# A two-layer graph network in one kernel: the transposes of the next tile behind a third of the present tile's products

## What is computed

```python
h = relu(layernorm(x))
x = x + gat(relu(gat(h, W1, ...)), W2, ...)     # graph attention, softmax over incoming edges
h = relu(layernorm(x))
x = x + gcn(relu(gcn(h, V1, ...)), V2, ...)     # graph convolution, normalized by degree
```

## Time and profile before

| what | value |
|---|---|
| median of 3 runs | 2283.92 us (2281.28 to 2285.07) |
| profiled execution: its time | 2278.45 us |
| profiled execution: its span | 2276.7 us |
| mean granted TensorE clock | 0.992 of full speed |
| TensorE (PE) busy | 2212.1 us, 97% |
| weight loads (PEld) busy | 1428.2 us, 63% |
| DVE busy | 1520.7 us, 67% |
| ACT busy | 935.1 us, 41% |
| POOL busy | 904.6 us, 40% |

### The profile page before, as it was taken

One profiled execution on the slowest core, in us unless ns is written; L12 is line 12 of the kernel. 1 busy time (PEld: TensorE's weight loads), 2 busy tenths in 40 slices (PEclk: granted clock), 3 DMA queues, 4 the chain that ended last, 5 costly groups with the idle time before them and its releaser, 6 DMA issues.

```text
span 2276.7 us, 36746 instructions
## 1 busy us (share of the span) xinstructions
PE 2212.1 (97%) x13888; PEld 1428.2 (63%) x13888; DVE 1520.7 (67%) x3352; ACT 935.1 (41%) x1291; POOL 904.6 (40%) x1071
## 2 busy tenths in 40 slices
PE   6999999999999999999999999999999999999997
PEld 3666666666666666666666666666665666666664
DVE  6888885444577776334589999766555657885564
ACT  3333433333455445433454444433333333333442
POOL 2332325754233331134455454444334423344562
PEclk8999999999999999999999999999999999999999
DMA  4433334565455554343565566676766657775562
GB/s 141 154 118 106 111 112 113 113 127 202 160 195 190 186 188 167 124 167 119 192 209 184 195 207 207 200 250 241 244 241 205 222 185 237 247 252 178 181 208 82
DMA packets 125668, 407.32 MB, mean 179 GB/s; under 512 B 21993, under 2 KB 22151, under 8 KB 125364
## 3 DMA queue, kind: packets, MB, share of 16 engines
q1 hardware_dynamic: 85124, 232.38, 30.5%
q0 software_dynamic: 40368, 172.60, 24.4%
HBM read 232.32 MB, written 179.87 MB: 181 GB/s over the span
## 4 chain that ended last, share of the span: by engine, by line
PE 80%; DVE 8%; POOL 4%; issue 4%; DMA 2%; ACT 2%; SPq 0%; POOLq 0%; ACTq 0%; DVEq 0%
PE ps_h L893 67%; PE ps_z L876 8%; DMA edge_mem<-rows,pos_dst 2%; PE ps_e L960 1%; PE ps_e L961 1%; DVE z_lo L1106 1%; DVE bn L1054 1%; POOL out L604 1%; DVE edge_mem L1136 1%; DVE res L1125 1%; ACT row_out L782 1%; POOL edge_mem L599 1%; DVE res L1115 1%; POOL rstd L613 1%; PE ps_e L968 0%
## 5 line engine op out<-in xcount | busy, mean ns | idle before, releaser
L893 PE MATMUL ps_h<-w_hi,z_hi 128*128 128x384 f16 x3792 | 928.4, 327 | 0.4 <-DVE w_lo L1045 0.4
L893 PE MATMUL ps_h<-w_lo,z_hi 128*128 128x384 f16 x3792 | 928.2, 327 | 0.0
L893 PE MATMUL ps_h<-w_hi,z_lo 128*128 128x384 f16 x3792 | 927.9, 326 | 0.0
L1106 DVE TENSOR_TENSOR z_lo<-ps_z,z_hi 128x768 f16<-128x768 f32 x316 | 301.7, 955 | 484.5 <-ACT z_hi L787 483.8
L893 PEld LDWEIGHTS ps_h<-w_lo,z_hi 128*128 128x128 f16 x3792 | 371.5, 98 | 246.4 <-issue 1.9
L893 PEld LDWEIGHTS ps_h<-w_hi,z_lo 128*128 128x128 f16 x3792 | 371.5, 98 | 246.0 <-issue 1.4
L893 PEld LDWEIGHTS ps_h<-w_hi,z_hi 128*128 128x128 f16 x3792 | 371.3, 98 | 223.6 <-issue 19.9
L782 ACT ACTIVATE row_out<-ps_h,grow 128x768 f32<-128x768 f32 x237 | 212.9, 898 | 637.7 <-PE ps_h L893 628.1
L876 PE MATMUL ps_z<-ident,z 128*128 128x128 f32 x1896 | 261.0, 274 | 24.8 <-ACT z L795 23.6
L611 POOL TENSOR_SCALAR veps<-mv 128x1 f32<-128x1 f32 x158 | 87.5, 554 | 457.2 <-DVE mv L1057 441.9
L787 ACT ACTIVATE z_hi<-ps_z 128x768 f16<-128x768 f32 x316 | 253.8, 803 | 15.4 <-PE ps_z L876 15.4
(11 more groups left out here) (213 smaller groups left out, 2131.1 us busy)
## 6 DMA issues: line engine op xcount, KB each, us to landing
rows<-row_out SPq DMA_DIRECT2D x199, 384.0 KB, 3.9
row_in<-in_x SPq DMA_DIRECT2D x78, 384.0 KB, 3.6
rows<-e_out SPq DMA_DIRECT2D x60, 384.0 KB, 4.5
row_in<-rows SPq DMA_DIRECT2D x40, 384.0 KB, 4.3
x_rows<-pre SPq DMA_DIRECT2D x40, 384.0 KB, 3.2
res<-x_rows SPq DMA_DIRECT2D x40, 384.0 KB, 4.1
pure_rows<-row_out SPq DMA_DIRECT2D x39, 384.0 KB, 3.5
row_in<-pure_rows SPq DMA_DIRECT2D x39, 384.0 KB, 4.6
```

What stands on the lines that cost most here:

```text
L893: last = nc.tensor.matmul(ps_h[s][:, a, 0:HALF], zp[s][:, c, :], wp[:, c, a * HALF:(a + 1) * HALF], start=(c == 0 and zp is z_hi and wp is ...
L1106: V.tensor_tensor(pair3(z_lo[t.slot]), psum_pair(ps_z), pair3(z_hi[t.slot]), ALU.subtract).then_inc(z_lo_ready, 1)
```

## The change

In `window(w)` of TensorE the call of `turn` for tile w+1 is taken from the front of the window and put into `side_step(0)`, which runs after chunk 1, so behind 12 of the 36 product matmuls of tile w. It stands ahead of all else that `side_step(0)` does. Only where a window has no product (w = -1) it stays in front. Nothing else is edited; ACT, DVE, POOL and SP have the same instructions in the same order.

```diff
             def window(w):
-                if t := tile(w, 1):
-                    turn(t)
                 gat = gat_of(w)
+                after = tile(w, 1)
+                if after and not tile(w, 0):
+                    turn(after)
 
                 def side_step(k):
+                    if after and k == 0:
+                        turn(after)
                     if ORDER <= w < ORDER + ET and k == 1:
                         mask_rows(w - ORDER)
```

## The result

| | before | after |
|---|---|---|
| median | 2284.49 us (4 runs, 2281.28 to 2285.3) | 2354.72 us (4 runs, 2353.89 to 2356.54) |
| ratio | | 1.031, 95% interval 1.029 to 1.033 |
| profiled execution: its time | 2278.45 us | 2354.51 us |
| profiled execution: its span | 2276.7 us | 2352.8 us |
| mean granted clock | 0.992 | 0.991 |

The changed kernel is 3.1% slower: 70 us by the medians, 76.1 by the spans of the two profiled executions. The work is the same; what came is nearly all waiting. Lines of the edited file from 931 on stand three higher than before (L948 is L951, L960 is L963, L968 is L971, L1106 is L1109).

The account below looks back on a forecast made before the run. TensorE, busy 97% of the span, was taken as the bound, so only waits could change. Stage terms summed to +70.5 us on the profiled 2278.45, giving 2349; the median stands 5.5 higher, so 2354, range 2325 to 2382.

Parts of the forecast that it names:

- Rank ring: Rank window pairs: 3.64 us to `z_lo`, 9.77 of DVE, 1.11 to products: 14.52 against 13.64; stage sum +17.8 us.
- The wait in window 28: Special rank pair: the 3.40 us wait for `z` becomes 1.7 without loss of clock; -3.6 us.
- Masks: 20 windows: the mask matmul's input follows `z_lo`, ready at 5.13 us, due at 4.56; wait 0.57 each, +11.4 us.
- First attention layer: 20 pairs, window B: slack before the matmul needing the weights falls from 2.1 to 0.6 us; cost 0 if that holds.
- Second attention layer: 20 pairs where DVE is full: cycle 15.93 us against 14.63 in nine pairs, others differ; +21 us, bounds +12 and +25.
- the recurrence: Second attention layer: DVE's cycle from window A's late `z_lo` to the next window, carried pair by pair; gives 22 us.
- Last edges: 20 windows, the first needing no copy: 19 waits of 0.67 us less some 1 us absorbed; +12 us.
- Plain edges: 20 windows: `carry` copies behind `z_hi` on ACT cost 0.7 us each, partly absorbed by old gather waits; +5.9, at most +14.
- Start: The second tile's transposes, which filled a wait for the first weights, now stand among the products; +0.9 us.
- The two other waits for `z`: Waits for `z` outside the other stages, 3.7 us: due 1.95 later, they fall by 0.9 and 1.95; -2.9 us.
- the weighing in the prediction: Skill's rule on short idles swinging TensorE's clock, set against waits of 1.23 and 1.65 us without half clock: trace disagrees.
- the rival of the falling clock: TensorE's clock falls in half of about 100 new waits, 2.7 us each: +135 more, 2490 us; chance 0.05.

Follow-up runs that it names:

- the second trace of the kernel before: The kernel before, unchanged, profiled once more at the end of the experiments; that execution took 2282.23 us.
- At two thirds: The changed kernel with the transposes behind 24 products, at `side_step(1)`, instead of 12; one execution of 2782.41 us.
- the dots-first kernel: The changed kernel with the first two dot products ahead of `low_parts` on DVE in window A of the second attention layer; span 2335.8 us.
- the carry-first kernel: The changed kernel with ACT's `carry` (plain edges) and `last_carry` ahead of `upper_parts`; span 2329.5 us.
- all reorderings: The changed kernel with `mask_diag`, statistics and two dot products ahead of `low_parts`, carries ahead of `upper_parts`, window 0's transposes in front; 2280.25 us, ratio 0.9986.
- Behind a sixth: Transposes behind 6 products in all windows but window 0, with the four queue reorderings, against the kernel before; 2281.61 us, ratio 0.9993.

## Why the prediction was right, point by point

**The sum.** +70.5 predicted on the profiled execution, +76.1 in the profiled execution after, +70 by the medians; 2354 us against 2354.72. That the last two agree to 1 us is luck: by the profiles I was 5.6 us short, and the two profiled executions stand at different distances from their medians (6.0 under, 0.2 under). Against the second trace of the kernel before the shift is 72.3.

**Rank ring: right.** 9.77 us of DVE and 3.64 us of lateness gave 14.52 a pair, measured 14.41. Statistics ahead of `low_parts` opened the ring. The wait in window 28 was worked out as 1.7 us, measured 1.55, without loss of clock, as forecast. Where the rows would show it I had partly wrong: L893 waits for `z_lo` 8 times and not 20, most of the pair's wait shows at L905.

**Masks: right in the wait, short in what hangs on it.** L913 starts 5.12 us into the window as worked out, but a window grew by 0.67 us, not 0.57. Start to start, L913 takes 0.54 us to the next product now (404.38 to 404.92) where it took 0.43 (357.47 to 357.90): its weights had been loaded while products ran, and now the load waits too. This row of the weight loads shows it, idle 0.79 us:

```profile
404.38 0.30 PEld L913 LDWEIGHTS ps_e<-diag,ones 128*128 128x128 f32 x2 [0.79 <-DVE diag L1284]
```

That is 20 x 0.11 = 2.2 us that the term left out; the term was mis-sized by 2.0, 13.4 against 11.4.

**First attention layer: right.** Expected 0, measured +0.1; the slack of 0.6 us held. At two thirds it was overdrawn, L951 waited up to 1.47 us a pair, but L920, which the prediction did not look at, waited 3.01.

**Second attention layer: right**, 21.3 against 21, and the dots-first kernel shows that the loss is in DVE's idle time at the `z_lo` of window A, which is what the recurrence said. That the two sizes agree is helped by one stretch at half clock, 1.7 us, which the term did not have.

**Last edges: right**, 12.6 against 12; the carry-first kernel takes all of it back, so ACT's order is the whole cause.

**Plain edges: right in the wait, not settled in size.** 6.6 against 5.9 by the first trace, but with the old order of ACT and the transposes in front this stage stood at 0, +3.4 and +5.5 in three executions, so the cost can be anything from 1 to 7 us. What is shown: every plain edge waits now, 20 waits of 12.3 us where 7 made 9.2, ACT no longer waits for the gathers there (0.2 us in place of 16.6), which is the absorption that I had assumed, and with the carries first the stage went to -1.9, and to -3.5 with all reorderings. Behind a sixth, or in front in all but three windows, the carries first left it at +6.0 and +5.5.

**Start: mis-sized**, +2.4 where the term said +0.9. I had counted the transposes alone, and not what the clock does to the products behind them. Before, the transposes of window 0 ran two microseconds ahead of the first products, and from 30.60 us on the products ran at full clock (two in 0.49 us):

```profile
26.97 1.54 PE L876 MATMUL ps_z<-ident,z 128*128 128x128 f32 x6 [16.48 <-ACT z L795]
...
30.60 0.49 PE L893 MATMUL ps_h<-w_hi,z_hi 128*128 128x384 f16 x2
```

In the changed kernel TensorE stands idle until the first weights come, and the products in front of the transposes all run at half clock,

```profile
29.07 0.80 PE L893 MATMUL ps_h<-w_hi,z_hi 128*128 128x384 f16 x2 [18.55 <-DVE w_lo L1048]
32.87 1.31 PE L876 MATMUL ps_z<-ident,z 128*128 128x128 f32 x6
```

so the twelve of them take 3.80 us, not 1.95, and the transposes 1.14 to the next product. Over all executions this stage is 1.6 us longer on average with window 0's transposes behind a third.

**The two other waits for `z`: wrong in size**, -1.5 together where I had -2.9. The step "1.95 later due, they fall by 0.9 and 1.95" took the supply of `z` to be fixed. In window 289 TensorE still waits 1.38 us, where with only three windows late it waits 0.82 and the window gives the 1.95 (against the second trace of before both gain 1.7 more, by the clock). In window 75 the supply moves further. POOL computes the degrees' root for 13.00 us (L707), behind the norm factors of a tile, which wait for DVE's statistics, which stand behind `low_parts`:

```profile
573.88 0.19 POOL L611 TENSOR_SCALAR veps<-mv 128x1 f32<-128x1 f32 x1 [5.25 <-DVE mv L1060]
...
575.03 13.00 POOL L707 TENSOR_TENSOR dinv<-perm_f,work 128x79 f32<-128x79 f32 x1
```

The held `z_lo` made DVE late and DVE made POOL late by 1.8 us: L707 starts 7.0 us into window 72, where it started 5.2 into it before (at 536.2). So TensorE waited 0.80 us instead of 0.95. With only window 75 late, nothing ahead of L707 is, L707 starts 5.2 us into window 72 again, and the whole 1.15 us comes back. That each link releases the next is read from the queues and not tested by itself.

**The clock.** The changed kernel has 110 short waits behind the start, of 0.2 to 2.5 us, and its mean granted clock is 0.991 against 0.992. Outside the start and the end half clock was granted three times for 3.4 us: behind a wait of 2.50 (L984, 343.5 us), one of 0.95 (361.5) and one of 2.52 (1382.01). The wait of 2.53 us shown above, at 1417.09, left the clock alone. The kernel before had two such places, from within the wait of 3.40 us on (for 6.8 us) and behind the 1.60 us of the earlier trace rows, and there the weighing in the prediction missed a row: it named the waits of 1.23 and 1.65 us that left the clock alone, and not this one. So the length of a wait alone does not decide it. The Trainium skill (TensorE: Matmul & The Clock Gate, "A second HAM failure mode") tells of a kernel in which frequent short idles between groups of matmuls made the clock swing between its levels. At one third this trace shows three swings in 110 waits, so the rival of the falling clock was wrong for this change; at two thirds, where TensorE waited 2.2 to 3.0 us in every mask window and every rank and attention pair, the trace agrees: 0.92 to 0.95 in the stretches.

## What to carry to other kernels

Before an instruction is moved back in one queue, write down for each engine what stands behind the instruction that it feeds, and when the first engine needs that: here TensorE waited for the late `z_lo` itself only 8 times, 6.4 us, and nearly all of the 76 us came from small work queued behind its consumers. A late producer costs by thresholds, not in proportion, so look for the few places with a real wait and move only there (the transposes made late in three windows gained some 6 to 8 us by the medians and the ratio, in all 315 they lost 70). And where an engine waits at the head of its queue for a late input, put independent work ahead of it: four such moves, with the first window left as it was, gave the whole loss back. How late a gather lands varies from execution to execution, so a stage that hangs on one is judged from more than one trace.

## What was not expected of the hardware

- A wait costs TensorE more than its row says. The idle time of the changed kernel sums to 50 us more than before, the span grew by 76. At the mask the row says 0.40 us, while the start of L913 slipped by 0.56 and it ran 0.11 longer start to start. The first difference is in how the rows are kept: a product's row lasts 0.33 us, though the next product starts 0.16 behind it, so the last row in front of a wait covers 0.16 of it. The second is the weight load, which is no longer hidden.
- 110 waits of 0.2 to 2.5 us, one in 7 to 16 us in the busy stages, left the mean clock at 0.991, with three stretches of 3.4 us at half. With 2.2 to 3.0 us per window or pair it was 0.92 to 0.95. And the same wait of 2.77 us was followed by half clock in one execution of the kernel before and not in the other.
- The same kernel's gathers in the plain stretch made TensorE wait 9.2 us in one execution and 11.0 in another, with the waits of every other edge matmul the same to 0.1 us.
